# When the first layer's expert weights are fetched: all at once ahead of unit 0, or in five parts beside unit 1

## The chip, the cores and the metric

One core of a Trainium2 chip runs the whole program. The metric is the device time of one execution in microseconds (us), lower is better. "Engine" below means TensorE (PE), VectorE (DVE), ScalarE (ACT), GpSimd (POOL) or SyncE (SP); SP only issues DMA transfers.

## The reference

Two transformer-like layers on x (8 batches of 256 tokens, 256 wide) with a context of 8 x 256 x 192:

- layer 0: x += tanh(g) * cross-attention(layernorm(x), context), 16 heads of 16; then x += tanh(g) * mixture(layernorm(x)), eight experts of inner width 128 of which a token uses four, and one shared expert: `silu(x Wg) * (x Wu) Wd`
- layer 1: the same cross-attention with its own weights, its scores clipped, and a check for NaN; then a mixture of eight experts of inner width 1024, two for each token

The weights that this change moves are layer 0's Wg, Wu and Wd for the eight experts and the shared one, its router's rows and correction bias, and layer 1's attention and router weights.

## The kernel before

Attention is worked through in 16 units, one for each layer and batch. Unit u's scores take eight slots of the program, one for each pair of heads; unit u begins at slot `base(u) = 18 + 8u`. In a slot PE computes one pair's scores by query (L693, `by_query`); DVE takes their row maxima (L1267, `rowmax`), and PE may not overwrite `by_query` before that. When the eight maxima of a unit are there, DVE makes a shift of them, PE turns it (L700), ACT copies it (L1069 and L1070, `shiftT`), and SP sends it on a round trip: `place_shift` stores it to DRAM (L518, `max<-shiftT`), waits, and loads it from there as two more rows of the unit's query stack (L523, `stack_q<-max`). Only then can PE compute that unit's scores by key (L712, `by_key`), ten slots (`LAG`) after its scores by query; ACT exponentiates them (L1077), and PE multiplies them with the values (L730). Projections, layer norms and layer 0's experts (PE L786, L796) of other units are put between these on the same in-order engines.

Before a unit starts, its keys and queries are stored to DRAM in two precisions (L474 and L477 for keys, L485 and L488 for queries; unit 0's queries go by ACT's queue) and loaded back by twelve transfers into stacks (L501 `stack_k<-qk`, L512 `stack_q<-qk`). PE's first `by_query` of a unit waits for them.

The order on each engine is a list written out by hand: `make_plan()` puts stages at half slots, and every engine walks the same plan. SP takes at slot g the stages of half slots 2g-3 and 2g-2, in order, and blocks where it must wait. Almost all DMA of this part is issued by SP, on one queue. SP's order around the change is:

```
slot 18  load(2): x and context of batch 3; all of layer 0's expert weights
slot 19  store of unit 1's queries        slot 21  store of context 2
slot 22  stacks of unit 1                 slot 23  store of unit 2's keys
slot 26  load(3): batch 4; layer 1's attention weights (8 transfers)
slot 27  place_shift(0), store of unit 2's queries
slot 29/30  context 3, stacks of unit 2   slot 31  store of unit 3's keys
slot 34  load(4): batch 5; layer 1's router weights and zero rows (7 transfers)
slot 35  place_shift(1), store of unit 3's queries
slot 37/38  context 4, stacks of unit 3   slot 39  store of unit 4's keys
slot 42  load(5)                          slot 43  place_shift(2), ...
```

`load_experts0` issues 12 transfers on `ffn0_in`: router rows (L425), bias (L426), four of gate and up weights with the shared expert's part behind each (L430, L431), down weights and the shared one (L432, L433). `gate_turn` (PE L765, ACT L1096) turns the router's rows and waits for all of them; it stands in slot 34, and the first experts' matmuls come in slot 44. PSUM banks for all such stages are handed out in turn over three banks, in the plan's order.

Of the kernel before, what the change touches and what calls it, by code (L numbers as in the profile page):

```python
# [21 lines left out]
P = 128  # L22
# [6 lines left out]
KC = D // P  # L29
E0, I0 = 8, 128  # L30
# [22 lines left out]
LAG = 10  # L53
# [12 lines left out]
def layer_of(u):  # L66
    return u // NB
# [6 lines left out]
def base(u):  # L74

    return LEAD + PAIRS * u


def make_plan():

    at = defaultdict(list)
    for u in range(UNITS):
        g = 2 * base(u)
        at[g - 34].append(("load", u))
        if u == 0:
            for i, stage in enumerate(FIRST):
                at[g - 30 + i].append(stage)
        else:
            at[g - 28].append(("ctx", u))
            at[g - 25].append(("kprod", u))  # L90
            at[g - 23].append(("stats", ("query", u)))
            at[g - 21].append(("normal", ("query", u)))
            at[g - 19].append(("turn", ("query", u)))
            at[g - 16].append(("qprod", u))
            at[g - 10].append(("stack_keys", u))
            at[g - 10].append(("stack_queries", u))
        at[g + 13].append(("vprod", u))
        at[g + 16].insert(0, ("shift_turn", u))
        e = g + 2 * LAG + 2
        at[e + 9].append(("take", 2 * u))  # L100
        at[e + 11].append(("turn_values", 2 * u))
        at[e + 17].append(("take", 2 * u + 1))
        at[e + 19].append(("turn_values", 2 * u + 1))
        at[e + 21].append(("attn_turn", u))
        at[e + 23].append(("project", u))
    at[2 * base(0)].append(("out_bias", 0))
    at[2 * base(NB) - 40].append(("scale_queries", 1))
    at[2 * base(2)].append(("gate_turn", 0))
    g = 2 * base(NB)
    at[g].append(("out_bias", 1))  # L110
    at[g + 6].append(("mean_v", 0))
    at[g + 10].append(("mean_turn", 0))
    at[g + 15].append(("mean_project", 0))
    for b in range(NB):
        e = 2 * base(0) + 2 * LAG + 25 + EXPERTS0_STEP * b
        at[e].append(("stats", ("ffn0", b)))
        at[e + 2].append(("normal", ("ffn0", b)))
        at[e + 5].append(("turn", ("ffn0", b)))
        at[e + 6].append(("route0", b))
        at[e + 8].append(("groups0", b))  # L120
        at[e + 9].append(("ranks0", b))
        at[e + 10].append(("weights0", b))
        for n in range(N0):
            at[e + 7 + EXPERTS0_STEP * n // N0].append(("gate_up", N0 * b + n))
            at[e + 12 + EXPERTS0_STEP * n // N0].append(("down0", N0 * b + n))
    g = 2 * base(UNITS - 1)
    at[g - 20].append(("load_alternative", 0))
    at[g - 13].append(("any_nan", 0))
    at[g - 11].append(("spread_nan", 0))
    for b in range(NB):  # L130
        g = 2 * base(UNITS - 1) - 9 + FINISH_STEP * b
        if b >= KEPT_FROM:
            g = max(g, 2 * base(NB + b) + 2 * LAG + 26)
        if b < KEPT_FROM:
            at[g - 9].append(("reload", b))
        at[g].append(("pick_z", b))
        at[g + 2].append(("stats", ("finish", b)))
        at[g + 4].append(("normal", ("finish", b)))
        at[g + 6].append(("turn", ("finish", b)))
        at[g + 8].append(("logits1", b))  # L140
        at[g + 9].append(("soft1", b))
        at[max(g + 10, 2 * base(UNITS) + 1 + b)].append(("count1", b))
        if b == NB - 1:
            at[g + 11].append(("blocks", 0))
            at[g + 12].append(("tables", 0))
        at[g + 11].append(("weights1", b))
        late = 5 if b == NB - 2 else 0
        at[g + 13 + late].append(("bias_turn", b))
        at[g + 15 + late].append(("bias1", b))
    return at  # L150
# [25 lines left out]
def bank_release(stage, n):  # L176

    if stage == "turn":
        return "xnT_ready", NORM_NO[n] + 1
    return {  # L180
        "gate_turn": ("gate_wT_ready", 1), "spread_nan": ("keep_ready", 1),
        "mean_v": ("mean_ready", 1), "mean_turn": ("mean_ready", 2), "mean_project": ("zalt_ready", 1),
    }.get(stage) or {
        "ctx": ("ctxT_ready", n + 1), "kprod": ("k_lo", n + 1), "qprod": ("q_lo", n + 1),
        "vprod": ("v_ready", n + 1), "out_bias": ("obias_ready", 2 * n + 2),
        "bias_turn": ("biasT_ready", n + 1), "bias1": ("x_done", n + 1),
        "shift_turn": ("shiftT_ready", n + 1), "turn_values": ("normal_done", n + 1),
        "attn_turn": ("attnT_ready", n + 1), "project": ("z_ready", n - NB + 1) if layer_of(n) else ("x0_ready", n + 1),
        "route0": ("sig_exp", n + 1), "gate_up": ("h_ready", n + 1), "down0": ("x_acc", n + 1),
        "logits1": ("logits_ready", n + 1),  # L190
    }[stage]


def share_banks():

    bank_of, uses = {}, []
    for g in sorted(PLAN):
        for stage, n in PLAN[g]:
            if stage in ("load", "stack_keys", "stack_queries", "stats", "scale_queries", "normal", "take", "groups0", "ranks0", "weights0", "any_nan",
                         "reload", "load_alternative", "pick_z", "soft1", "count1", "weights1", "blocks", "tables") or (stage == "ctx" and layer_of(n)):  # L200
                continue
            i = len(uses)
            bank_of[stage, n] = (i % 3, bank_release(*uses[i - 3]) if i >= 3 else None)
            uses.append((stage, n))
    return bank_of


BANK_OF = share_banks()


def build(nc, a, out):
    es = ExitStack()
    first = ExitStack()
    sem = Semaphores(*[es.enter_context(nc.semaphore(name)) for name in SEMAPHORES])
# [5 lines left out]
    def sba(name, shape, dt=F32):  # L220
        return first.enter_context(nc.sbuf_tensor(name, shape, dt))
# [50 lines left out]
    w_gate0 = sba("w_gate0", [P, KC, N0, I0])  # L272
    w_up0 = sba("w_up0", [P, KC, N0, I0])
    w_down0 = sba("w_down0", [P, N0, D])
    gate_wT = sba("gate_wT", [P, KC, E0])
    corr = sba("corr", [P, E0])
# [25 lines left out]
    gate_rows = hidden0[2][0:E0, :]  # L302
# [90 lines left out]
    def _(sp):  # L393
        def load_x(b):
            sp.dma_start(x_tiles(b), a["x"][b].rearrange("(t p) d -> p t d", p=P)).then_inc(x_in[b], 16)
# [25 lines left out]
                    sp.dma_start(dst, col.rearrange("(k p) -> p k", p=P),  # L421
                                 allow_slow_non_contiguous=True).then_inc(attn_w_in[l], 16)

        def load_experts0():
            sp.dma_start(gate_rows, a["L0_ffn_gate_w"]).then_inc(sem.ffn0_in, 16)  # L425
            sp.dma_start(corr[:, :], a["L0_ffn_correction_bias"].partition_broadcast(P)).then_inc(sem.ffn0_in, 16)  # L426
            for k in range(KC):
                rows = slice(k * P, k * P + P)
                for t, w, shared in ((w_gate0, a["L0_ffn_Wg"], a["L0_ffn_Wg_s"]), (w_up0, a["L0_ffn_Wu"], a["L0_ffn_Wu_s"])):
                    sp.dma_start(t[:, k, 0:E0, :], w[:, rows, :].rearrange("e p i -> p e i")).then_inc(sem.ffn0_in, 16)  # L430
                    sp.dma_start(t[:, k, E0, :], shared[rows, :]).then_inc(sem.ffn0_in, 16)  # L431
            sp.dma_start(w_down0[:, 0:E0, :], a["L0_ffn_Wd"].rearrange("e i d -> i e d")).then_inc(sem.ffn0_in, 16)  # L432
            sp.dma_start(w_down0[:, E0, :], a["L0_ffn_Wd_s"]).then_inc(sem.ffn0_in, 16)  # L433

        def load_router():
            sp.dma_start(wr[:, :, :], a["L1_ffn_Wr"].rearrange("(k p) e -> p k e", p=P)).then_inc(sem.router_in, 16)
# [18 lines left out]
        def load(u):  # L455
            if layer_of(u):
                reload_context(u)
            if u == 0:
                load_attention_weights(0)
            if u + 1 < NB:  # L460
                load_x(u + 1)
                load_ctx(u + 1)
            if u == 2:
                load_experts0()
            if u == 3:
                load_attention_weights(1)
            if u == 4:
                sp.wait_ge(sem.const, 1)
                load_router()

# [111 lines left out]
        def store_rows(b):  # L582
# [4 lines left out]
        load_x(0)  # L587
        load_ctx(0)
        stages = {"load": load, "ctx": context, "kprod": store_keys, "qprod": store_queries, "stack_keys": stack_keys, "stack_queries": stack_queries,
                  "shift_turn": place_shift, "mean_project": store_alternative, "project": store_z, "reload": reload, "load_alternative": load_alternative,  # L590
                  "weights1": store_rows, "bias1": store_x, "tables": first_weights}
        for g in range(SLOTS_IN_ALL):
            u, p = divmod(g - base(0) - LAG, PAIRS)
# [1201 lines left out]
```

## Time and profile before

| | |
|---|---|
| median of 3 runs | 1070.68 us (1070.47 to 1071.9) |
| the profiled execution | 1065.39 us, its span 1063.6 us |
| busy share of the span | PE 87%, DVE 71%, ACT 46%, POOL 22% |
| mean granted clock of PE | 0.896 of full speed |
| bytes moved | 142.03 MB, mean 134 GB/s |

The profiled execution is one of those of the kernel, 5.3 us under the median of the timed ones; about 1.8 us of it lies outside the span. Shares are averages over stages with different limits; the change moves work that lies in the first 160 us.

### The profile page before, as it was taken

What the parts mean: (1) busy time and instruction counts of PE and PEld (TensorE: products, weight loads), DVE (VectorE), ACT (ScalarE), POOL (GpSimd) and SP (SyncE); (2) the same over time, 40 slices, a digit from 0 to 9 for tenths busy, and PEclk for the clock granted to TensorE, in tenths of its full rate; (3) what the DMA queues carried; (4) which work ended last, traced back from release to release, by engine and by line L of the source; (5) the groups of instructions that cost most, each with busy time, mean ns of one, the idle gap of its engine ahead of it and who ended that gap; (6) DMA issues with size and microseconds to landing.
All of it is one profiled execution on the core that took longest, in us unless ns stands there. A gap on an engine that the chain in (4) does not pass through costs nothing.

```text
span 1063.6 us, 17907 instructions
## 1 busy us (share of the span) xinstructions
PE 922.6 (87%) x6385; PEld 736.5 (69%) x6385; DVE 754.2 (71%) x1489; ACT 486.1 (46%) x842; POOL 235.0 (22%) x386
## 2 busy tenths in 40 slices
PE   3568999999999999898897676785489999999995
PEld 2345677777777676676665444553389999999995
DVE  3634667777667678788867578963768888888882
ACT  2125644444444444334343333442256676667762
POOL 2011211020210000201010122421135444454423
PEclk9557999999999999899998766865589999999998
DMA  6996746056055116365462874341366776677742
GB/s 151 265 176 140 132 78 109 23 95 103 31 84 84 31 55 123 94 120 107 128 124 91 161 150 111 93 131 40 110 239 209 233 233 220 202 227 236 230 140 30
DMA packets 121080, 142.03 MB, mean 134 GB/s; under 512 B 11456, under 2 KB 105304, under 8 KB 120864
## 3 DMA queue, kind: packets, MB, share of 16 engines
q1 hardware_dynamic: 110512, 128.11, 48.5%
q0 software_dynamic: 8832, 12.25, 5.3%
q8 instruction: 51, 0.84, 0.3%
q10 hardware_dynamic: 1648, 0.53, 0.2%
q14 instruction: 37, 0.30, 0.1%
HBM read 109.97 MB, written 30.88 MB: 132 GB/s over the span
## 4 chain that ended last, share of the span: by engine, by line
PE 62%; DVE 14%; DMA 10%; SPq 4%; issue 4%; ACT 3%; POOL 2%; ACTq 0%; POOLq 0%; DVEq 0%
PE bank L947 12%; PE bank L786 8%; PE by_key L931 6%; PE by_query L931 6%; PE bank L796 5%; PE value_bank L730 4%; DVE rowmax L1267 3%; PE by_query L693 3%; PE by_key L712 3%; DMA max<-shiftT 3%; PE bank L640 3%; PE bank L757 3%; PE bank L679 2%; DVE probs L1292 2%; PE bank L649 2%
## 5 line engine op out<-in xcount | busy, mean ns | idle before, releaser
L1267 DVE TENSOR_REDUCE rowmax<-by_query 128x4 f32<-128x1024 f32 x128 | 155.5, 1215 | 27.2 <-PE by_query L693 27.0
L1077 ACT ACTIVATE probs<-by_key 128x1024 f32<-128x1024 f32 x128 | 130.7, 1021 | 66.6 <-PE by_key L712 63.8
L1721 POOL TENSOR_SCALAR rstd<-moments 128x2 f32<-128x2 f32 x32 | 9.6, 300 | 545.6 <-DVE moments L1231 545.6
L1772 POOL DMA_INDIRECT out_x<-x,token_i x46 | 78.2, 1700 | 146.6 <-ACT x L1182 136.6
L693 PE MATMUL by_query<-stack_k,stack_q 48*128 48x256 f32 x512 | 71.0, 359 | 38.3 <-DVE rowmax L1267 20.6
L947 PE MATMUL bank<-w_hi,h_hi 128*128 128x256 f32 x368 | 104.1, 283 | 0.0
L947 PE MATMUL bank<-w_lo,h_hi 128*128 128x256 f32 x368 | 104.1, 283 | 0.0
L947 PE MATMUL bank<-w_hi,h_lo 128*128 128x256 f32 x368 | 104.1, 283 | 0.0
L693 PEld LDWEIGHTS by_query<-stack_k,stack_q 48*128 48x128 f32 x512 | 43.6, 210 | 77.3 <-issue 46.1
L1110 ACT ACTIVATE act_gate<-bank 128x256 f32<-128x256 f32 x72 | 27.6, 383 | 142.4 <-PE bank L786 140.0
L712 PE MATMUL by_key<-stack_q,stack_k 50*128 50x256 f32 x512 | 66.8, 342 | 29.2 <-DMA stack_q<-max 26.3
L1292 DVE SCALAR_TENSOR_TENSOR probs<-probs,lower 128x1024 f32<-128x1024 f32 x64 | 77.8, 1215 | 14.0 <-DMA lower<-max 10.6
L796 PE MATMUL bank<-w_down,hidden 128*128 128x256 f32 x288 | 80.4, 403 | 3.1 <-DVE summed L1324 1.8
L730 PE MATMUL value_bank<-probs,values 128*32 128x256 f32 x1024 | 78.3, 429 | 5.2 <-DVE probs L1292 5.0
L712 PEld LDWEIGHTS by_key<-stack_q,stack_k 50*128 50x128 f32 x512 | 43.6, 209 | 55.9 <-DMA stack_q<-max 28.6
L786 PE MATMUL bank<-xnT,w_gate 128*128 128x256 f32 x288 | 80.0, 401 | 1.7 <-DVE lo L1258 0.5
L1419 DVE SCALAR_TENSOR_TENSOR x<-bank,expert_cols,x 128x256 f32<-128x256 f32 x144 | 62.5, 475 | 21.0 <-PE bank L796 20.9
L786 PE MATMUL bank<-xnT,w_up 128*128 128x256 f32 x288 | 75.9, 387 | 0.0
L947 PEld LDWEIGHTS bank<-w_hi,h_hi 128*128 128x128 f32 x368 | 70.7, 192 | 0.0
L947 PEld LDWEIGHTS bank<-w_lo,h_hi 128*128 128x128 f32 x368 | 70.7, 192 | 0.0
L947 PEld LDWEIGHTS bank<-w_hi,h_lo 128*128 128x128 f32 x368 | 70.7, 192 | 0.0
L1649 DVE TENSOR_TENSOR h_lo<-x,h_hi 128x512 fp32r<-128x512 f32 x92 | 63.7, 693 | 3.2
(228 smaller groups left out, 2141.4 us busy)
## 6 DMA issues: line engine op xcount, KB each, us to landing
w<-in_L_ffn_W SPq DMA_DIRECT2D x46, 1024.0 KB, 8.7
lower<-max SPq DMA_DIRECT2D x64, 256.0 KB, 3.8
stack_k<-qk SPq DMA_DIRECT2D x96, 128.0 KB, 5.0
stack_q<-qk SPq DMA_DIRECT2D x96, 128.0 KB, 7.4
qk<-hi SPq DMA_DIRECT2D x31, 256.0 KB, 3.5
qk<-lo SPq DMA_DIRECT2D x31, 256.0 KB, 4.1
rows<-w_gate SPq DMA_DIRECT2D x8, 264.0 KB, 3.6
x<-in_x SPq DMA_DIRECT2D x8, 256.0 KB, 8.0
```

Source lines behind the costliest of these rows:

```text
L693: mm = pe.matmul(by_query[:, side, t * S:t * S + S], sq[rows, p, t * P:t * P + P], sk[rows, p, :], start=True, stop=True)
L712: mm = pe.matmul(by_key[:, side, kt * S:kt * S + S], sk[rows, p, kt * P:kt * P + P], sq[rows, p, :], start=True, stop=True)
L730: mm = pe.matmul(value_bank[32 * c:32 * c + 32, o:o + S], values[u % 2][:, kt, 4 * j + c, :], probs[(i + c // 2) % 4][:, kt, c % 2, :], st ...
L786: mm = pe.matmul(bank[:, half * S:half * S + S], w[:, k, e, :], turned_of(("ffn0", b))[:, k, :], start=k == 0, stop=k == 1)
L796: mm = pe.matmul(bank[:, t * D:t * D + D], hidden0[i % 6][:, t * P:t * P + P], w_down0[:, e, :], start=True, stop=True)
L931: mm = pe.matmul(up_bank[pair][:, half * SLOTS:half * SLOTS + SLOTS], wt[:, k, j * P:j * P + P], xt[:, k, :], start=n == 0, stop=n == len( ...
L947: mm = pe.matmul(bank[:, t * D:t * D + D], ht[:, j, t * P:t * P + P], wt[:, j, :], start=j == 0 and t == 0 and n == 0, stop=j == JH - 1 an ...
L1077: ac.activation(probs[i % 4][:, :, :, :].rearrange("p k h s -> p h k s"), by_key[:, :, :].rearrange("p h (k s) -> p h k s", k=2), ACT.Exp) ...
L1267: dv.tensor_reduce(rowmax[u % 2][:, 2 * p:2 * p + 2, :], by_query[:, :, :].rearrange("p h (t s) -> p h t s", t=TT), AX, ALU.max).then_inc( ...
L1292: dv.scalar_tensor_tensor(prob, prob, 1.0, bound, ALU.min, ALU.max).then_inc(sem.clip_done, 1)
L1649: dv.tensor_tensor(hl[:, part, :], relu[pair], hh[:, part, :].bitcast(F32), ALU.subtract).then_inc(sem.h_lo, 1)
L1772: po.indirect_dma_start(out[:, :], bass.IndirectOffsetOnAxis(ap=token_i[:, n:n + 1].bitcast(U32), axis=0), ysb[i % 3][:, t, :], None, comp ...
```

## The change

`load_experts0` becomes five parts: gate weights for each half of the rows (part 0 also brings the router's rows and the bias), up weights for each half, down weights. They are put at half slots 59, 61, 63, 65 and 67, so that SP issues them in its slots 31 to 35: part 0 behind the store of unit 3's keys, part 3 ahead of `load(4)`, part 4 ahead of `place_shift(1)`. `gate_turn` goes from half slot 68 to 85. Layer 1's attention weights go from `load(3)` to `load(5)`, its router weights from `load(4)` to `load(6)`.

```diff
     at[2 * base(NB) - 40].append(("scale_queries", 1))
-    at[2 * base(2)].append(("gate_turn", 0))
+    g = 2 * base(1) + 7
+    for i in range(5):
+        at[g + 2 * i].append(("load_experts0", i))
+    at[2 * base(0) + 2 * LAG + 25 + 4].append(("gate_turn", 0))
...
-        def load_experts0():
-            sp.dma_start(gate_rows, a["L0_ffn_gate_w"]).then_inc(sem.ffn0_in, 16)
-            sp.dma_start(corr[:, :], a["L0_ffn_correction_bias"].partition_broadcast(P)).then_inc(sem.ffn0_in, 16)
-            for k in range(KC):
+        def load_experts0(i):
+
+            if i == 0:
+                sp.dma_start(gate_rows, a["L0_ffn_gate_w"]).then_inc(sem.ffn0_in, 16)
+                sp.dma_start(corr[:, :], a["L0_ffn_correction_bias"].partition_broadcast(P)).then_inc(sem.ffn0_in, 16)
+            if i < 2 * KC:
+                up, k = divmod(i, KC)
                 rows = slice(k * P, k * P + P)
...
+                t, w, shared = ((w_up0, a["L0_ffn_Wu"], a["L0_ffn_Wu_s"]) if up else (w_gate0, a["L0_ffn_Wg"], a["L0_ffn_Wg_s"]))
+                sp.dma_start(t[:, k, 0:E0, :], w[:, rows, :].rearrange("e p i -> p e i")).then_inc(sem.ffn0_in, 16)
+                sp.dma_start(t[:, k, E0, :], shared[rows, :]).then_inc(sem.ffn0_in, 16)
+            else:
+                sp.dma_start(w_down0[:, 0:E0, :], a["L0_ffn_Wd"].rearrange("e i d -> i e d")).then_inc(sem.ffn0_in, 16)
+                sp.dma_start(w_down0[:, E0, :], a["L0_ffn_Wd_s"]).then_inc(sem.ffn0_in, 16)
...
-            if u == 2:
-                load_experts0()
-            if u == 3:
+            if u == 5:
                 load_attention_weights(1)
-            if u == 4:
+            if u == 6:
                 sp.wait_ge(sem.const, 1)
                 load_router()
```

The rest of the diff lets `load_experts0` be a stage of SP's list and of none that takes a PSUM bank.

## Rows read from the trace of the kernel before

**Rows 1.** Stretches: length, busy time (count) of PE, PEld, DVE, ACT, POOL; PEclk, DMA share, GB/s.

```profile
24.00:27.00 3.00, 0.00 (x0) 0.00 (x0) 2.15 (x7) 0.22 (x1) 0.62 (x3) 0.97 1.16 129
27.00:30.00 3.00, 0.00 (x0) 0.00 (x0) 2.54 (x2) 1.03 (x2) 1.53 (x6) 0.50 1.13 127
39.00:46.00 7.00, 4.51 (x22) 2.78 (x22) 4.49 (x7) 1.67 (x6) 0.00 (x0) 0.74 1.17 290
48.00:51.00 3.00, 1.88 (x7) 0.83 (x6) 0.81 (x3) 0.84 (x2) 0.00 (x0) 0.50 1.11 366
69.00:70.00 1.00, 0.00 (x0) 0.00 (x0) 0.83 (x3) 0.05 (x1) 0.00 (x0) 1.00 0.36 44
78.00:86.00 8.00, 6.05 (x35) 4.03 (x37) 4.09 (x8) 2.86 (x5) 1.05 (x3) 0.50 1.15 139
88.00:91.00 3.00, 3.00 (x7) 2.45 (x8) 0.84 (x1) 1.58 (x3) 0.71 (x1) 0.50 1.07 343
125.00:150.00 25.00, 24.68 (x164) 18.06 (x161) 18.55 (x52) 11.38 (x22) 3.36 (x9) 1.00 0.69 133
```

**Rows 2.** The chain that ended last, from 26 us on: start, us, what.

```profile
30.43 1.90 SPq L425
...
45.54 7.31 DMA qk<-lo
...
55.11 8.50 DMA stack_q<-qk
...
65.22 5.64 DMA max<-shiftT
```

**Rows 3.** SP's DMA issues in order of time (start, us to issue).

```profile
45.06 0.43 SPq L485 DMA_DIRECT2D qk<-hi  x1
...
70.87 1.36 SPq L523 DMA_DIRECT2D stack_q<-max  x2
...
74.46 2.79 SPq L501 DMA_DIRECT2D stack_k<-qk  x6
...
82.60 0.38 SPq L477 DMA_DIRECT2D qk<-lo  x1
...
87.37 0.64 SPq L442 DMA_DIRECT2D out_x<-zero_row  x1
95.19 0.50 SPq L518 DMA_DIRECT2D max<-shiftT  x1
97.02 1.26 SPq L523 DMA_DIRECT2D stack_q<-max  x2
...
121.31 0.51 SPq L518 DMA_DIRECT2D max<-shiftT  x1
```

**Rows 4.** PE, and one row of DVE, in order of time (in brackets: idle before, releaser).

```profile
30.20 1.08 PE L670 MATMUL bank<-ident,xn 128*128 128x128 f32 x4 [6.92 <-ACT xn L1043]
55.10 3.78 PE L649 MATMUL bank<-wkv,ctxT 96*128 96x256 f32 x8
60.50 1.23 DVE L1267 TENSOR_REDUCE rowmax<-by_query 128x4 f32<-128x1024 f32 x1 [4.06 <-PE by_query L693]
63.71 0.80 PE L693 MATMUL by_query<-stack_k,stack_q 48*128 48x256 f32 x4 [3.25 <-DMA stack_q<-qk]
74.24 0.79 PE L712 MATMUL by_key<-stack_q,stack_k 50*128 50x256 f32 x4 [1.20 <-DMA stack_q<-max]
101.31 0.50 PE L712 MATMUL by_key<-stack_q,stack_k 50*128 50x256 f32 x4
114.99 1.89 PE L649 MATMUL bank<-wkv,ctxT 96*128 96x256 f32 x8
128.83 0.50 PE L712 MATMUL by_key<-stack_q,stack_k 50*128 50x256 f32 x4
```

**Rows 5.** DMA issues by line up to 150 us: count, KB each, median us to landing.

```profile
w_gate<-in_L_ffn_Wg SPq DMA_DIRECT2D x2, 512.0 KB
...
w_down<-in_L_ffn_Wd SPq DMA_DIRECT2D x1, 1024.0 KB
```

More of the change, by code:

```diff
@@ L199, in share_banks @@
             if stage in ("load", "stack_keys", "stack_queries", "stats", "scale_queries", "normal", "take", "groups0", "ranks0", "weights0", "any_nan",
-                         "reload", "load_alternative", "pick_z", "soft1", "count1", "weights1", "blocks", "tables") or (stage == "ctx" and layer_of(n)):
+                         "reload", "load_experts0", "load_alternative", "pick_z", "soft1", "count1", "weights1", "blocks", "tables") or (stage == "ctx" and layer_of(n)):
                 continue
@@ L422, in load_attention_weights @@
                                  allow_slow_non_contiguous=True).then_inc(attn_w_in[l], 16)
-        def load_experts0():
-            sp.dma_start(gate_rows, a["L0_ffn_gate_w"]).then_inc(sem.ffn0_in, 16)
-            sp.dma_start(corr[:, :], a["L0_ffn_correction_bias"].partition_broadcast(P)).then_inc(sem.ffn0_in, 16)
-            for k in range(KC):
-                rows = slice(k * P, k * P + P)
[L429 to L433, printed above, removed]
+        def load_experts0(i):
[4 more added lines that the diff above has]
+                up, k = divmod(i, KC)
+                rows = slice(k * P, k * P + P)
+                t, w, shared = ((w_up0, a["L0_ffn_Wu"], a["L0_ffn_Wu_s"]) if up else (w_gate0, a["L0_ffn_Wg"], a["L0_ffn_Wg_s"]))
[4 more added lines that the diff above has]
+                sp.dma_start(w_down0[:, E0, :], a["L0_ffn_Wd_s"]).then_inc(sem.ffn0_in, 16)
         def load_router():
@@ L589, in _ @@
         stages = {"load": load, "ctx": context, "kprod": store_keys, "qprod": store_queries, "stack_keys": stack_keys, "stack_queries": stack_queries,
-                  "shift_turn": place_shift, "mean_project": store_alternative, "project": store_z, "reload": reload, "load_alternative": load_alternative,
+                  "shift_turn": place_shift, "mean_project": store_alternative, "project": store_z, "reload": reload, "load_experts0": load_experts0, "load_alternative": load_alternative,
                   "weights1": store_rows, "bias1": store_x, "tables": first_weights}
```

## The prediction, as it was put on record

> **What bounds the kernel now.** I read the stretches first, then the chain of waits over the first 130 us, then SP's issues and PE's instructions in order of time. From 125 us on PE is busy 24.68 of 25 us at the full clock [rows 1]: a delay or gain that reaches that point is carried to the end one for one, so only the first 130 us need a sum. There the chain runs through SP and DMA [rows 2]: SP issues expert weights from 30.43 us; the store of unit 1's queries goes out only at 45.06 and 45.54, and its second part takes 7.31 us to land; the query stacks then take 8.50 us. PE begins unit 1's scores at 63.71 after 3.25 us of waiting for them [rows 4]. The shift's first trip takes 5.64 us [rows 2] against 97.02 - 95.19 = 1.83 us for the next unit's [rows 3], and PE waits 1.20 us more for it at 74.24 [rows 4].
>
> The DMA engines have two rates [rows 1]: 139 GB/s while the stacks are loaded (78 to 86 us), 290 where gate and up weights pass (39 to 46), 343 to 366 for transfers of longer rows (88 to 91, 48 to 51). A transfer of one queue that is issued behind others lands behind them.
>
> **What the change removes.** Nothing reaches unit 0's scores: its stacks were issued before the experts. Behind it:
>
> 1. Unit 1's stacks. Their issue no longer stands behind 12 transfers; PE and DVE of unit 0 do not speed up. PE may start unit 1 when DVE has read the last scores of unit 0: 60.50 + 1.23 = 61.73, say 61.9 against 63.71 [rows 4]. Gain 1.8 us, not the 3.25 that PE shows, because DVE is next to be late. The stacks, issued from about 45 us and needing about 13 (unit 2's: 74.46 to some 87, from rows 1 and 3), land near 58 and cover this.
> 2. Unit 0's shift. Issued at 65.22 - 1.8 = 63.4, with no layer 1 weights ahead of it: 1.83 us to land, then from L523 to `by_key` 74.24 - 70.87 = 3.4 [rows 3, 4], so 68.7. PE comes there at 74.24 - 1.20 - 1.8 = 71.2. The 1.20 us goes too: gain so far 3.0 us at slot 28.
>
> Left alone, PE would reach unit 1's first `by_key` (101.31 before, no wait shown [rows 4]) at 98.3, and its shift would be ready for L518 at about 95.19 - 3.0 = 92.2 [rows 3].
>
> **What it adds, step by step.** The 12 issues now come behind unit 3's key store (82.60 before [rows 3]) and ahead of `place_shift(1)`. Before, SP had only the router's seven transfers there and was idle from 88.0 to 95.19 [rows 3]. The data is the larger part:
>
> - Unit 2's stacks are issued at 74.46 - 1.8 = 72.6 (they hang on context 3, ahead of the 1.20 us) and passed in 12.5 us before, until about 87 [rows 1, 3]. So the queue reaches what is behind them at 85.1.
> - Ahead of L518 then lie: unit 3's keys, 0.52 MB; x and context 5, 0.46 MB; gate and up, 4 x (512 + 64) KB = 2.36 MB; down, 1152 KB = 1.18 MB (sizes [rows 5] and the arrays' shapes). 2.36 MB at 290 GB/s is 8.1 us, 2.16 MB at 350 is 6.2 us: 14.3 us, until 99.4.
> - The shift's store lands behind that. The nearest pattern is unit 0's in the kernel before: the queue ran empty at about 69.2 (share 0.36 in 69 to 70 [rows 1]) and `by_key` started at 74.24: 5.0 us. So unit 1's `by_key` starts at 104.4, against 101.31: **+3.1 us**. Bounds: 4.52 MB at 366 with 3.4 us behind it gives 100.9 (-0.4); all at 290 with 5.0 gives 105.7 (+4.4).
> - SP itself has issued the last part some us before its data has passed and is not later than this. While it waits for the shift's store, unit 3's query store, context 4 and unit 3's stacks stand behind it. Before, L523 of unit 1 went out at 97.02; now at about 101. The stacks then land at about 118 us, unit 3 begins at about 122 to 124: covered by 4 us, else late by the excess.
> - PE is in order: while `by_key` waits, from 98.3 to 104.4, unit 2's next scores and unit 4's key projection wait too. The idle time also bears on the clock. Before, PE idled 6.92 us until 30.20 [rows 4]; the granted clock was 0.97 in 24 to 27 and 0.50 (1.2 GHz) in 27 to 30, and it was still 0.50 in 78 to 86 and 88 to 91 with PE busy 6.05 of 8 and 3.00 of 3 us [rows 1]. At that level the eight matmuls of L649 take 3.78 us, at the full clock 1.89 [rows 4]. A 6 us stall at 98 us should bring the fall again. Cost: nothing if the clock holds; at most half of the 9.05 us busy in those two stretches, 4.5 us. I take half of some 3.2 us: **+1.6 us**.
>
> **Costed at nothing.** Layer 1's attention weights in `load(5)`: about 1.06 MB, 3 us of DMA, ahead of unit 2's shift. L518 of that unit went out at 121.31 and its `by_key` ran at 128.83; the round trip takes 1.83 + 3.4 = 5.2, so 2.3 us of cover, and the queue should be empty by 124.5 when the shift comes at 126. Without cover it costs up to 3 us. The router's transfers in `load(6)` fall in the next unit, where DMA is busy 0.69 of the time [rows 1]. `gate_turn`'s own instruction only moves; its weights have landed 15 us earlier. Its PSUM bank is freed at once, and the turn of the first expert input now waits for an older neighbour: at worst a fraction of a microsecond.
>
> **Sum.** -3.0 (two waits gone) + 6.1 (new wait at `by_key`) = +3.1; +1.6 clock; together +4.7 us, bounds -0.4 and +8.9. The profiled execution of 1065.39 us becomes 1070.1; the median of the timed runs lies 5.3 us above it, so 1075.4 us.
>
> **Rivals.**
>
> A, faster: the shift's small store does not wait its turn behind the experts, or SP gets to it before. Then the 3.0 us stays: 1067.7 us. It would need L518's data to pass 3.6 MB already in the queue. Against it: with the layer 1 weights ahead, the same store took 5.64 us instead of 1.83 [rows 2, 3], and unit 1's query store 7.31. It decides if the landing comes before 98.3 - 3.4 = 94.9 us. A page of the Trainium skill, "DMA: Bandwidth & Descriptors", section "Queues, rings and completion order", says that a copy is split over up to 16 engines' rings and that completion is not first in, first out for an issuing engine; by it a later small transfer could land first, which gives this case's 1067.7 us, though the same section has each engine take descriptors in ring order, which gives mine. The two landings just named agree with the latter. Chance 0.17.
>
> B, no change: unit 1's shift is late by only what the front gained: the transfers pass at 366 GB/s and the landing is quick (100.9 to 102 us), and the clock holds. The time stays within 2 us of 1070.7. For it: the bound above, and PE's clock could rise sooner in 62 to 92 us. That would bring unit 2's stacks out sooner, but not what follows the stall. Chance 0.23.
>
> C, the forecast, +2 to +9 us, mostly near +4.7. Chance 0.52.
>
> D, slower by more: unit 3's stacks or unit 2's shift also come too late, each a further 2 to 4 us with a second fall of the clock: 1080 to 1084. It decides if L518 of unit 1 lands after 103 us. Chance 0.08.
>
> **How the numbers follow.** What a measurement of this kernel can tell from no change is about 0.2%, 2.1 us. Faster by more: case A, 0.17. Within: case B, 0.23. Slower: C and D, 0.60. The predicted time is C's 1075.4; C alone lies in 1073 to 1079.5. The range for 8 in 10 leaves out most of A below and D above: 1068 to 1080.
>
> **What the profile of the changed kernel would show.** Right: no wait for `stack_q<-qk` at unit 1's first scores, which start near 61.9; the first `by_key` near 71.2 without a wait; DMA share near 0.2 or less in parts of 38 to 45 us; weight issues from about 80 to 93; a wait of about 6 us of L712 for `stack_q<-max` that ends near 104; a granted clock of 0.50 around or behind it. Wrong: L518 of unit 1 landing within 2 us of its issue, or no wait at slot 36 (then A); unit 1's first scores well before 61.9 would mean that something in unit 0 hung on DMA that I missed; a clock at the full level after the stall makes it +3. A wait at unit 2's `by_key` or unit 3's first scores would be D.

## The result, and the profile after

| | before | changed |
|---|---|---|
| median of 20 runs each | 1069.56 us (1061.1 to 1075.66) | 1073.33 us (1068.98 to 1079.12) |
| the profiled execution | 1065.39 us, span 1063.6 | 1077.79 us, span 1076.0 |
| ratio of the times | | 1.0043, 95% interval [1.0023, 1.0064] |

By the ratio the change makes the kernel 0.43% slower, some 4.6 us (2.5 to 6.8 by the interval); the two medians lie 3.8 us apart. The two profiled executions differ by 12.4 us, more than the timed runs do, so part of that is chance of the single execution, and it has to be told apart below.

In the changed kernel the lines lie five further down for TensorE's and ScalarE's stages: L698 is the scores by query, L717 the scores by key, L523 and L528 SP's shift trip. First PE in order of time (brackets: idle before, releaser). The rows answer to [rows 4].

```profile
62.10 0.80 PE L698 MATMUL by_query<-stack_k,stack_q 48*128 48x256 f32 x4 [1.42 <-DVE rowmax L1272]
...
71.15 0.79 PE L717 MATMUL by_key<-stack_q,stack_k 50*128 50x256 f32 x4
...
98.16 0.64 PE L629 MATMUL bank<-ident,ctx_tok 128*96 128x128 f32 x4
104.84 0.80 PE L717 MATMUL by_key<-stack_q,stack_k 50*128 50x256 f32 x4 [6.03 <-DMA stack_q<-max]
...
109.40 3.78 PE L645 MATMUL bank<-ctxT,wkv 96*128 96x256 f32 x8
...
127.62 0.30 PE L705 MATMUL bank<-ident,shift 128*96 128x128 f32 x1
```

Unit 1's first scores start at 62.10 in place of 63.71, released by DVE; the first `by_key` runs at 71.15 in place of 74.24, without a wait. Then PE stands still for 6.03 us at unit 1's first `by_key`, which before ran at 101.31 with no wait.

SP's issues in order of time, against [rows 3]:

```profile
72.63 2.77 SPq L506 DMA_DIRECT2D stack_k<-qk  x6
...
80.00 0.47 SPq L430 DMA_DIRECT2D hidden<-in_L_ffn_gate_w  x1
...
93.35 1.34 SPq L440 DMA_DIRECT2D w_down<-in_L_ffn_Wd_s  x1
94.73 0.66 SPq L523 DMA_DIRECT2D max<-shiftT  x1
101.55 1.23 SPq L528 DMA_DIRECT2D stack_q<-max  x2
...
129.31 0.51 SPq L523 DMA_DIRECT2D max<-shiftT  x1
```

The weights fill SP from 80.00 to 94.7; the shift's store is issued right behind and lands 6.82 us later (101.55), where it took 1.83 us before. SP also came to the store late: PE turned this shift at 91.91 us, and in the kernel before SP issued the store 0.70 us behind the turn (94.49 to 95.19), so that 2.1 us of the trip's delay passed before the issue and 5.0 us behind it. The stretches (columns as in [rows 1]) show what the DMA engines and the clock did meanwhile:

```profile
38.00:40.00 2.00, 1.60 (x7) 1.03 (x5) 1.95 (x4) 0.84 (x2) 0.00 (x0) 0.88 0.00 0
70.00:73.00 3.00, 2.38 (x14) 1.57 (x12) 1.80 (x2) 1.66 (x5) 0.00 (x0) 0.50 0.00 0
77.00:84.00 7.00, 5.05 (x36) 2.69 (x36) 4.09 (x8) 2.89 (x4) 1.74 (x7) 0.50 1.16 142
88.00:94.00 6.00, 5.83 (x45) 3.85 (x43) 2.86 (x5) 3.03 (x5) 0.00 (x0) 0.86 1.16 292
95.00:99.00 4.00, 3.03 (x33) 1.65 (x32) 3.32 (x6) 1.95 (x3) 0.00 (x0) 1.00 0.98 298
99.00:104.00 5.00, 0.00 (x0) 0.00 (x0) 0.50 (x1) 0.76 (x4) 0.00 (x0) 0.93 0.14 46
104.00:120.00 16.00, 13.51 (x76) 8.41 (x76) 5.84 (x11) 5.54 (x7) 1.65 (x6) 0.50 1.11 212
122.00:130.00 8.00, 7.83 (x59) 5.82 (x57) 4.73 (x11) 5.09 (x10) 2.14 (x8) 1.00 0.27 54
```

The DMA engines are now empty in 38 to 40 and in 70 to 73 us, where nothing uses them, and full from 77 to 99. From 104 to 120 PE runs at the lower level, 1.2 GHz. The eight matmuls of L645 at 109.40 take 3.78 us there; in the kernel before the same stage is L640, at the full clock:

```profile
104.72 1.99 PE L640 MATMUL bank<-ctxT,wkv 96*128 96x256 f32 x8
```

A mark that can be compared from one execution to the next is the start of a unit's shift turn on PE. Unit 3's, in the two profiled executions of each kernel (the second pair was taken later; lines differ by one):

```profile
157.36 0.32 PE L700 MATMUL bank<-ident,shift 128*96 128x128 f32 x1
```
```profile
161.87 0.31 PE L701 MATMUL bank<-ident,shift 128*96 128x128 f32 x1
```
```profile
165.95 0.32 PE L705 MATMUL bank<-ident,shift 128*96 128x128 f32 x1
```
```profile
162.07 0.32 PE L706 MATMUL bank<-ident,shift 128*96 128x128 f32 x1
```

These are before, before again, changed, changed again. The same program reaches this mark 4.5 us or 3.9 us apart in two executions. The means, 159.6 and 164.0, differ by 4.4 us; a single pair of profiles would have said 8.6 or 0.2. With two executions of each kernel, that 4.4 is close to the timed 4.6 is luck and no evidence. The same turns of later units show how far the mark reaches (all in us):

| shift turned | before | before again | changed | changed again |
|---|---|---|---|---|
| unit 1 | 94.49 | 98.75 | 91.91 | 90.36 |
| unit 2 | 119.61 | 124.13 | 127.62 | 123.73 |
| unit 3 | 157.36 | 161.87 | 165.95 | 162.07 |
| unit 9 | 416.95 | 421.46 | 425.54 | 421.65 |
| unit 15 | 680.30 | 682.70 | 691.91 | 687.56 |

From unit 3 to unit 9 all four take 259.6 us, so that a delay of the front is carried on unchanged that far; the prediction had it unchanged to the end. From unit 9 to unit 15 they take 263.4, 261.2, 266.4 and 265.9 us, at a mean granted clock of 0.86, 0.87, 0.85 and 0.85 (420 to 690 us). Two further runs told of below, the 46 matmuls of 48 rows and the shift on ScalarE's queue, have the changed kernel's plan in this stretch and take 262.8 and 262.5 us. So no cost of the change is shown there; it is a second source of scatter, of some 6 us over all profiles.

### The profile page after: what moved, and what is told of

It is laid out like the page before. It is cut to its first block, busy times and chain, and to the rows that moved or that the text cites. A ratio compares the mean times of both kernels' runs of the same rounds, so it can differ in the third digit from the quotient of the medians.

```text
span 1076.0 us, 17907 instructions
## 1 busy us (share of the span) xinstructions
PE 934.7 (87%) x6385; PEld 744.3 (69%) x6385; DVE 754.1 (70%) x1489; ACT 486.4 (45%) x842; POOL 234.3 (22%) x386
## 4 chain that ended last, share of the span: by engine, by line
PE 63%; DVE 15%; DMA 8%; issue 4%; SPq 4%; ACT 3%; POOL 2%; ACTq 0%; POOLq 0%; DVEq 0%
PE bank L952 12%; PE bank L791 8%; PE by_key L936 6%; PE by_query L936 6%; PE bank L801 5%; PE bank L645 4%; PE value_bank L735 4%; DVE rowmax L1272 3%; PE by_query L698 3%; DMA max<-shiftT 3%; PE by_key L717 3%; PE bank L762 3%; PE bank L684 2%; DVE probs L1297 2%; PE bank L654 2%
## 5 line engine op out<-in xcount | busy, mean ns | idle before, releaser
L1272 DVE TENSOR_REDUCE rowmax<-by_query 128x4 f32<-128x1024 f32 x128 | 155.5, 1215 | 32.5 <-PE by_query L698 32.3
L698 PE MATMUL by_query<-stack_k,stack_q 48*128 48x256 f32 x512 | 72.4, 365 | 32.3 <-DVE rowmax L1272 21.0
L717 PE MATMUL by_key<-stack_q,stack_k 50*128 50x256 f32 x512 | 67.8, 347 | 34.8 <-DMA stack_q<-max 31.5
L698 PEld LDWEIGHTS by_query<-stack_k,stack_q 48*128 48x128 f32 x512 | 44.7, 215 | 71.6 <-issue 41.3
L717 PEld LDWEIGHTS by_key<-stack_q,stack_k 50*128 50x128 f32 x512 | 44.6, 213 | 61.8 <-DMA stack_q<-max 33.6
```

The lines of the kernel that those rows point to most:

```text
L698: mm = pe.matmul(by_query[:, side, t * S:t * S + S], sq[rows, p, t * P:t * P + P], sk[rows, p, :], start=True, stop=True)
L717: mm = pe.matmul(by_key[:, side, kt * S:kt * S + S], sk[rows, p, kt * P:kt * P + P], sq[rows, p, :], start=True, stop=True)
L1272: dv.tensor_reduce(rowmax[u % 2][:, 2 * p:2 * p + 2, :], by_query[:, :, :].rearrange("p h (t s) -> p h t s", t=TT), AX, ALU.max).then_inc( ...
```

## The experiments

Each was compared with the kernel before on the same chip. The table's last column is the mark just told; both marks are from one execution each, and scatter as above.

| run | ratio to before, 95% interval | unit 1's first `by_key` | unit 3's shift turned |
|---|---|---|---|
| changed | 1.0043 [1.0023, 1.0064] | 104.84 | 165.95 |
| 46 matmuls of 48 rows in the wait | 1.0067 [1.0040, 1.0094] | 101.86 | 165.53 |
| shift on ScalarE's queue | 1.0081 [1.0055, 1.0108] | 104.81 | 165.75 |
| down weights behind the shift | 0.9997 [0.9973, 1.0020] | 100.61 | 164.16 |
| weights in DMA's gaps | 0.9961 [0.9940, 0.9983] | 95.19 | 156.33 |
| 24 matmuls of 128 rows | 1.0038 [1.0008, 1.0067] | 107.42 | 166.53 |
| gaps, and 12 such matmuls | 1.0004 [0.9980, 1.0027] | 96.94 | 156.21 |
| layer 1's weights alone | 0.9978 [0.9950, 1.0007] | 100.37 | 156.42 |
| all five parts behind the shift | 1.0024 [0.9994, 1.0053] | 95.80 | 161.59 |
| 12 matmuls of 128 rows | 1.0050 [1.0027, 1.0073] | 104.80 | 163.43 |
| gaps, layer 1's weights as before | 0.9980 [0.9949, 1.0010] | 100.82 | 157.46 |

### The data ahead of the shift: down weights behind it

```diff
-    g = 2 * base(1) + 7
-    for i in range(5):
-        at[g + 2 * i].append(("load_experts0", i))
+    for i, g in enumerate((59, 61, 63, 65, 69)):
+        at[g].append(("load_experts0", i))
```

> The changed kernel with part 4 alone (the down weights, 1.18 MB) moved from ahead of unit 1's shift to one slot behind it. Theory (the wait is the data ahead of the shift): 1.18 MB at 290 to 350 GB/s is 3.4 to 4 us less, so by_key starts near 101.3 us after a wait of some 2.5 us; whether the clock still falls is open (2.5 us is shorter than the idle time before the fall at 103); unit 2's shift near 119 to 121, the time 1067 to 1070. Rival (the wait comes from SP reaching the shift late, 94.7 against 92.2 us): by_key moves by no more than those 2.5 us, to 102.3 or later.

```profile
100.61 0.80 PE L716 MATMUL by_key<-stack_q,stack_k 50*128 50x256 f32 x4 [4.80 <-DMA stack_q<-max]
```

From the first issue of unit 2's stacks (72.01 us) to L528's counterpart (97.49) it is 25.5 us, against 28.9 and 27.3 in the two profiles of the changed kernel (72.63 to 101.55, 73.35 to 100.67): 1.8 to 3.4 us less for 1.18 MB less. The wait is 4.80 us and not 2.5, because PE came to it earlier, at 95.8 us, in an execution whose clock had risen sooner. The time is that of the kernel before. Both theories put `by_key` near what came, so its start does not tell them apart; the interval and the time go with the data. SP's own delay is not excluded as a part of the wait: it issued this store at 93.20 us, some 3.6 us after it could have (the shift was turned at 88.93). The clock fell here too, at 98 us, with 4.80 us of waiting.

### Everything behind the shift

```diff
-    g = 2 * base(1) + 7
     for i in range(5):
-        at[g + 2 * i].append(("load_experts0", i))
+        at[69].append(("load_experts0", i))
```

> The changed kernel with all five parts behind unit 1's shift and unit 3's query store, ahead of context 4 and unit 3's stacks. Theory (whatever stands behind 3.5 MB in SP's queue is late by its 11 to 12 us, less its cover): unit 1's first by_key does not wait; unit 3's stacks land 11 to 12 us later than they would, and unit 3's first scores by query wait for stack_q some 3 to 4 us. The front's 3 us are spent again: ratio 0.998 to 1.003. Rival (only the shift's round trip is so sensitive): no wait at unit 3, ratio 0.994 to 0.997.

```profile
121.23 0.57 PE L697 MATMUL by_query<-stack_k,stack_q 48*128 48x256 f32 x4 [3.27 <-DMA stack_q<-qk]
```

Unit 1's `by_key` does not wait (95.80 us), and unit 3's first scores wait 3.27 us for their stacks, as the sum said. The 3.5 MB cost whoever stands behind them. The clock fell here as well, in 97 to 98 us, with no DMA wait of PE ahead of it. The ratio's interval includes 1.

### Another queue for the shift

In place of SP, ScalarE issues unit 1's store and, once it has landed, the two loads:

```diff
+            if u == 1:
+                ac.wait_ge(sem.shiftT_ready, 2)
+                ac.dma_start(max_dram[0][1, 0:2 * H * TT], shiftT[0:2 * H * TT, :]).then_inc(sem.shift_out, 16)
+                ac.wait_ge(sem.shift_out, 32)
...
+                    ac.dma_start(stack_q[1][o:o + 2, :, :].bitcast(F32), src[side]).then_inc(sem.shift_in, 16)
```

> The changed kernel, with unit 1's shift trip (the store and the two loads) issued by ScalarE on its own queue in place of SP's; the expert weights are where the change put them. Theory (the shift waits its turn behind 4.5 MB in SP's queue, as in order of issue): on another queue it lands within 2 to 3 us although the expert weights still pass, unit 1's first by_key starts near 99 us with less than 2 us of waiting, no fall of the clock, unit 2's shift is turned at 117 to 119 us, and the time is 1065 to 1068. ScalarE stands still for some 3 to 4 us meanwhile. Rival (the bandwidth itself is short, whatever the queue): the store still takes 5 to 7 us, by_key starts near 104 us or later, and the time is 1073 or more.

```profile
92.16 0.60 ACTq L1080 DMA_DIRECT2D max<-shiftT  x1
96.75 1.81 ACTq L1085 DMA_DIRECT2D stack_q<-max  x2
```

The store took 4.59 us: 2.2 less than on SP's queue behind the weights, 2.8 more than the 1.83 of an empty queue. So both were half right: the order of the queue is one part, the other is that the same DMA engines are full. The Trainium skill ("DMA: Bandwidth & Descriptors", section "Queues, rings and completion order") has each DMA engine take turns between queues. The 4.59 us are in agreement with it: a store that is shortened on its own queue and not freed. This trip did not hold up unit 1's `by_key`, but ScalarE stood still from 92.8 to 98.7 us and with it PE's previous pair (5.47 us for `probs`), so the stall only changed its place. The clock fell at 99.7 us, and the ratio is the highest of all runs.

### The clock

Four runs put work into the wait or near it; the matmuls write the bank that the next `by_key` overwrites. In the first three PE's wait for ScalarE's exponentials, which read that bank, is moved ahead of the wait for the shift, so that the extra work comes between the two.

```diff
+            if u == 1 and p == 0:
+                for n in range(46):
+                    pe.matmul(by_key[:, 0, 0:S], sk[0:FULL, p, 0:P], sq[0:FULL, p, :], start=True, stop=True)
```

> This is the changed kernel with 46 extra matmuls in slot 36, into the by_key bank that unit 1's first scores by key overwrite anyway, so that PE works while it waits for unit 1's shift; nothing else moves. My theory (a 6 us wait for the shift, and the fall of the clock behind it costs about as much again): the wait's end stays near 104.8 us, the granted clock stays at the full level from 90 us on, unit 2's shift is turned near 123.3 us in place of 127.6, some 4 us earlier, and the time is 1069 to 1070 against 1073.3 (ratio to before 0.999 to 1.000). Rival (the clock falls for another reason, the light load of slots 36 to 38): the clock falls all the same behind the extra work, unit 2's shift is turned near 127 us, and the time stays at 1073.

```profile
94.00:96.00 2.00, 2.00 (x19) 2.00 (x18) 0.39 (x1) 0.65 (x4) 0.00 (x0) 0.94 0.96 298
96.00:98.00 2.00, 2.00 (x11) 2.00 (x11) 0.00 (x0) 0.00 (x0) 0.00 (x0) 0.50 0.31 104
...
110.00:116.00 6.00, 5.09 (x37) 3.16 (x36) 4.61 (x10) 2.89 (x4) 0.88 (x3) 0.50 1.13 212
```

PE was busy without a gap and the clock fell all the same, at 96 us, while 48-row matmuls ran. My expectation failed; unit 2's shift was turned at 127.19 us, as the rival had it. Then with 128 rows of the array in use (`wq` by `wo`), 24 of them. They differ from the first kind in a second thing: the stacks are declared float32r, `wq` and `wo` plain float32, and the trace has one instruction for a matmul of the first kind and two for one of the second. Which of the two decides on the clock was not tried.

> The changed kernel with 24 extra matmuls of 128 rows and 128 columns by 256 in slot 36, where the earlier try had 46 of 48 rows, which did not hold the clock. If it is the kind of load that the clock answers to, it stays at the full level through the wait and beyond 104 us, unit 2's shift is turned 29 us or less behind the end of the wait less some 6 (near 123.5 us where it was 127.6 and 127.2), and the time is 3 to 4 us under the changed kernel's: ratio to before 1.000 to 1.002. Rival (the clock falls at that moment whatever PE does): a fall at 96 to 103 us, unit 2's shift near 127, ratio 1.004 to 1.008 as with the 48-row matmuls.

```profile
96.00:98.00 2.00, 1.95 (x13) 1.71 (x14) 1.23 (x2) 0.75 (x4) 0.00 (x0) 1.00 0.45 150
98.00:104.00 6.00, 6.00 (x29) 5.28 (x29) 0.00 (x0) 0.08 (x1) 0.00 (x0) 1.00 0.53 155
104.00:110.00 6.00, 5.07 (x38) 3.85 (x40) 1.23 (x1) 1.31 (x2) 0.00 (x0) 1.00 1.14 159
110.00:116.00 6.00, 4.16 (x38) 2.88 (x32) 2.39 (x5) 3.08 (x5) 0.00 (x0) 1.00 0.81 154
116.00:122.00 6.00, 6.00 (x41) 3.97 (x38) 3.45 (x7) 3.54 (x5) 3.35 (x9) 0.57 0.94 261
```

The clock stayed at the full level to 116 us. But I had priced a matmul at 0.24 us, and each is two of the trace's, 10.53 us for the 24: they ended at 107.4. The shift's store had landed at 98.39, and `by_key` can follow that by 3.3 us (101.55 to 104.84 in the changed kernel), so the matmuls outlasted the wait by some 5.7 us, and that ate what the clock gave. The clock then fell at 117 us, and the ratio, 1.0038, is not what I expected. With half as many (`range(12)`):

> The changed kernel with 12 of the 128-row matmuls in slot 36. With 24 the clock stayed at the full level through the wait, but they took 10.53 us and outlasted it by some 5.5 us. Twelve take 5.3 us, less than the wait. Theory (the wait's empty time brings the fall): full clock until 110 us or later, unit 1's by_key at 101.7 to 104.8 us as the landing has it, unit 2's shift turned 18.5 to 21 us behind it (22.8 and 20.0 in the two profiles of the changed kernel), ratio 0.999 to 1.002 against 1.0043. Rival: the fall comes all the same, ratio 1.003 or more.

```profile
98.00:104.00 6.00, 2.90 (x14) 2.21 (x12) 0.00 (x0) 0.00 (x0) 0.00 (x0) 1.00 0.34 110
104.00:110.00 6.00, 4.44 (x30) 2.56 (x31) 1.22 (x1) 2.48 (x3) 0.00 (x0) 0.52 1.09 213
110.00:116.00 6.00, 4.16 (x32) 3.06 (x31) 2.72 (x6) 1.91 (x4) 0.00 (x0) 0.91 1.15 151
```

They filled 5.35 us; 3.90 us of wait were left, and at 104 us the clock fell, but was back at 111. From `by_key` to unit 2's shift turn it is 20.3 us (104.80 to 125.10), as expected, but the clock did not stay at the full level until 110 us, and the timed ratio, 1.0050, is not better than the changed kernel's. So what the fall costs in the timed runs is not shown.

To see whether the fall belongs to the change at all, both kernels were profiled again, unchanged.

> The kernel before once more, unchanged, for a second profile. Open after the first runs: the granted clock fell at 96 to 103 us in all five profiles of kernels with the experts moved, with a wait or without, and not in the one profile of the kernel before. If the fall belongs to those kernels, it is absent here too: unit 2's shift is turned 25.1 us behind unit 1's, as in the first profile. Rival (it belongs to the light load of slots 36 to 38, and the first profile escaped it by the moment of its earlier rise): the clock falls here as well in slots 36 to 38, and unit 2's shift is turned 28 to 30 us behind unit 1's.

> The changed kernel once more, unchanged, for a second profile. Theory (the wait is fixed by the data in SP's queue): unit 1's first by_key starts 32 to 32.5 us behind the first issue of unit 2's stacks (32.2 in the first profile) after a wait of some 6 us, whatever the clock did before. The fall of the clock behind it is expected again; how long it lasts (17 us in the first profile) may differ by one step of 3 to 4 us.

In the kernel before the clock did not fall in slots 36 to 38 this time either, with its light load there: before, unit 2's shift came 25.1 us behind unit 1's, now 25.4 (98.75 to 124.13). But it had risen late, at 99 us, where it rose at 91 in the first profile. That is only a part of the 4.5 us that this execution is behind the first: 2.0 us were there at unit 0's first scores (36.44 against 34.44) and 2.3 at unit 1's (65.99 against 63.71).

```profile
96.00:98.00 2.00, 2.00 (x20) 0.58 (x16) 1.49 (x4) 1.02 (x1) 0.00 (x0) 0.50 0.00 0
98.00:104.00 6.00, 5.69 (x47) 4.06 (x47) 3.06 (x6) 3.02 (x7) 0.00 (x0) 0.88 0.09 25
```

In the changed kernel, the wait was there again, 6.46 us, 30.35 us behind the first stack issue (32.2 in the first profile). I had expected 32 to 32.5, so the data passed 1.9 us faster than the theory of a fixed time allows:

```profile
103.70 0.80 PE L718 MATMUL by_key<-stack_q,stack_k 50*128 50x256 f32 x4 [6.46 <-DMA stack_q<-max]
```

and the clock was down for some 10 us (99.3 to 109.5) where it had been 17 (103.3 to 120.4). Of the 3.9 us between the two marks, 1.1 are the earlier `by_key` and 2.8 the way from there to unit 2's shift turn, which holds the shorter fall.

### Layer 1's weights alone

The kernel before, with only `u == 3` and `u == 4` in `load` made 5 and 6.

> The kernel before with layer 1's attention and router weights alone moved two units later; the expert weights stay at once ahead of unit 0. Theory (the two waits of the front have separate causes): PE's wait for unit 1's query stacks stays (unit 1's first scores near 63.7 us), the first trip of the shift takes 2 us in place of 5.64, the first by_key starts 1.2 us earlier with no wait; unit 1's by_key does not wait. Time 1 us under before, ratio 0.997 to 1.000. Rival (moving them costs something at unit 2's shift): a wait of L717's counterpart at unit 2, or no gain at all.

```profile
63.82 0.80 PE L693 MATMUL by_query<-stack_k,stack_q 48*128 48x256 f32 x4 [3.27 <-DMA stack_q<-qk]
...
73.26 0.80 PE L712 MATMUL by_key<-stack_q,stack_k 50*128 50x256 f32 x4
```

The wait for unit 1's stacks is unchanged, the shift's store lands in 1.87 us (65.32 to 67.19), and the 1.20 us wait is gone. The two waits of the front have separate causes, one for each half of the change. The ratio's interval, 0.9950 to 1.0007, just includes 1.

### The weights in DMA's gaps

```diff
-    g = 2 * base(1) + 7
-    for i in range(5):
-        at[g + 2 * i].append(("load_experts0", i))
+    for i, g in enumerate((37, 37, 47, 55, 69)):
+        at[g].append(("load_experts0", i))
```

> The changed kernel with the five parts where its trace shows the DMA engines idle: parts 0 and 1 at half slot 37 (behind the store of unit 1's queries, 41 to 45 us), part 2 at 47 (ahead of 60 us), part 3 at 55 (behind unit 2's query store, 69 to 72 us), part 4 at 69 (behind unit 1's shift). Theory: the 3.0 us of the front are kept (unit 1's first scores at 62 us, the first by_key at 71.2 without a wait), unit 1's first by_key starts near 98.3 us without a wait for the shift, no fall of the clock, unit 2's shift is turned near 117 us (119.6 before, 127.6 changed), and the time is about 3 us under before: 1066 to 1067, ratio 0.996 to 0.998. Rival (the early transfers hold up unit 1's stacks again): a wait at 62 us and half or less of the gain, unit 2's shift at 118.5 or later.

Its stretches (PE to GB/s as above):

```profile
38.00:46.00 8.00, 5.28 (x23) 3.55 (x23) 4.33 (x7) 1.67 (x6) 0.00 (x0) 0.71 0.53 149
66.00:71.00 5.00, 2.68 (x16) 2.07 (x16) 3.23 (x4) 0.89 (x6) 0.00 (x0) 0.50 0.76 223
92.00:97.00 5.00, 3.51 (x36) 2.00 (x36) 3.77 (x6) 2.96 (x7) 0.00 (x0) 1.00 0.78 228
...
98.00:104.00 6.00, 6.00 (x28) 3.55 (x30) 0.00 (x0) 1.98 (x3) 0.00 (x0) 0.50 1.14 194
```

The stretches that were empty now carry the weights; unit 1's first scores start at 61.60 and its first `by_key` at 95.19, neither with a DMA wait. It is the fastest version: 0.9961 [0.9940, 0.9983] against before, some 4 us. Its interval overlaps that of layer 1's weights alone (0.9978), so what the expert weights add to the gain is not told by time. I expected no fall of the clock, and it fell, at 97 us, with no DMA wait ahead of it; the mark is at 156.33 in spite of that. Here the matmuls with which the clock had stayed up were tried as well, three ahead of each of unit 1's first four `by_key`:

> The kernel with the weights in DMA's gaps (ratio 0.996), with three extra matmuls of 128 rows ahead of each of unit 1's first four by_key pairs, where PE waits some 0.3 to 0.9 us for ScalarE. They cost at most 12 x 0.24 = 2.9 us at the full clock, some of it inside waits. If the load of slots 36 to 38 decides on the clock, it no longer falls at 97 us and unit 2's shift is turned 26 to 28 us behind unit 1's (29.6 without them): 1 to 3 us gained, ratio 0.993 to 0.996. Rival (no hold on the clock): it falls all the same, the extra work costs 3 to 6 us, ratio 0.998 to 1.001.

Unit 2's shift was turned 29.0 us behind unit 1's (29.6 without them), the mark stayed (156.21) and the timed ratio was 1.0004: they cost what they gave or more. But the clock did not fall. The same stage without them and with them, and a stretch with them:

```profile
99.76 3.78 PE L644 MATMUL bank<-ctxT,wkv 96*128 96x256 f32 x8
```
```profile
101.56 1.99 PE L644 MATMUL bank<-ctxT,wkv 96*128 96x256 f32 x8
98.00:104.00 6.00, 5.37 (x39) 3.60 (x39) 0.95 (x1) 2.55 (x4) 0.00 (x0) 1.00 1.13 202
```

The granted clock was full from 85 to 128 us. The clock had risen at 83 to 84 us in both. So, as far as one execution of each shows, a load of this kind in slots 36 to 39 keeps this fall away. The fall's price can be read too: 29.6 us from turn to turn with it, 25.1 and 25.4 in the kernel before without it, some 4.2 to 4.5 us. The twelve matmuls took 6.1 us of PE.

With layer 1's weights put back where the kernel before has them:

> The kernel with the parts in DMA's gaps (ratio 0.9961), but layer 1's attention and router weights where the kernel before has them (units 3 and 4's loads). Theory: the attention weights (1.06 MB, issued ahead of unit 0's shift) delay that shift as before, and part 3, which used the gap at 67 to 71 us, comes on top; the first by_key waits 1 to 3 us; the router's small transfers cost nothing. Ratio 0.998 to 1.000, some 1 to 3 us over the version with both moved. Rival (layer 1's weights do not matter): ratio 0.995 to 0.997.

```profile
73.65 0.80 PE L716 MATMUL by_key<-stack_q,stack_k 50*128 50x256 f32 x4 [3.03 <-DMA stack_q<-max]
```

The first `by_key` waits 3.03 us, as the theory had it, and the ratio is 0.9980, with an interval that includes 1. It also overlaps the interval of the version with both moved, so the time alone does not show what layer 1's weights cost. This run has the experts moved, and the clock did not fall; unit 2's shift came 25.2 us behind unit 1's:

```profile
98.00:104.00 6.00, 4.70 (x56) 2.71 (x56) 4.18 (x6) 3.35 (x7) 0.00 (x0) 1.00 0.86 273
```

So the fall does not belong to every kernel with the experts moved. Six profiles have no extra work and no wait of PE of a microsecond or more in slots 35 to 38. In four of them (before, before again, layer 1's weights alone, this one) the clock had risen at 90 to 99 us and did not fall in slots 36 to 38; in two (the weights in DMA's gaps, all five parts behind the shift) it had risen at 83 to 84 us and fell at 97. The changed kernel's front, which brings PE to these slots earlier, may bring the fall by that; no run shows it alone.

## Why the prediction was right, point by point

- **Unit 1's stacks, 1.8 us, not 3.25.** 61.9 forecast, 62.10 measured, and DVE was what released it. The step that mattered was to ask what is late next.
- **Unit 0's shift.** First `by_key` at 71.2 forecast, 71.15 measured; the run with layer 1's weights alone shows which half of the change did it.
- **The new wait.** Forecast from 98.3 to 104.4; measured from 98.8 to 104.84, and to 103.70 in the second profile. Queue order and full engines both enter: on its own queue the store still took 4.59 us. The prediction told of queue order only, and its sum, drain of the queue at 99.4 us and then 5.0 us, was right for the pair of them: the DMA share is 0.98 until 99 us and 0.14 behind it, and `by_key` follows that by some 5.5 us in the first profile and 4.3 in the second. From the first issue of unit 2's stacks to the landing it takes 27.3 to 29.2 us in the five profiles with this placement and SP's queue, whenever PE arrives; a PE that comes earlier only waits longer.
- **-3.0 + 6.1 = +3.1.** At unit 1's `by_key`: 104.84 and 103.70 against 101.31 in the first profile of before, +3.5 and +2.4. Against the second profile of before (105.82) it is less than nothing, since there the clock had risen late; the timed runs, not a pair of profiles, carry the sign. The 3.0 us of the front rest on the first profile of before in the same way: at unit 1's shift turn the changed kernel is 2.6 to 8.4 us ahead, by the pair that is taken.
- **The clock, +1.6.** The fall came where forecast, and its bound was 4.5 us. No row gives the 3.2 us of which the prediction took half. In the first profile it lasted 17 us and L645 took 3.78 us against 1.99 before (L640); from `by_key` to unit 2's shift turn it took 22.8 us there and 20.0 in the second, against 18.3 in both of before (101.31 to 119.61, 105.82 to 124.13): +4.5 and +1.7. But the reason that I gave, idle time, is not the whole one: the clock also fell with PE busy on 48-row matmuls, and in two versions without a DMA wait. With matmuls of `wq` by `wo` in these slots it stayed up, so the kind of load enters; the rise at 83 to 84 or at 90 us and later may enter too. Twelve such matmuls in the wait shortened the fall without a gain in the timed runs. What the term is worth in those, and what brings the fall in the changed kernel, stays open.
- **Unit 3.** Forecast to begin at 122 to 124; its first scores by query start at 127.18 and 123.29 in the two profiles, without a wait for its stacks. The later one is that with the long fall of the clock.
- **Costed at nothing.** Layer 1's weights at unit 2: `by_key` waits for them in no run, but the cover was used: the shift's store took 3.5 us with layer 1's weights alone and 3.6 with twelve matmuls in the wait, against 1.84 in the changed kernel. `gate_turn`: from unit 2's shift turn to unit 3's it is 37.75 us before (119.61 to 157.36) and with layer 1's weights alone, and 38.33 in the changed kernel; its own instruction now lies in this stretch (0.29 us), and the turn of the first expert input waits 0.30 us for DVE. So it costs 0.6 us, the fraction of a microsecond that was named.
- **The rivals.** A did not come: the small store did wait. B did not come either: the store landed at 101.55, `by_key` at 104.84 and 103.70 was behind B's 100.9 to 102, and the clock fell. D's first mechanism did not come in the change, but is real: with all parts behind the shift, unit 3's stacks were 3.27 us late.
- **The size.** +4.7 us forecast, +0.43% of 1069.56 = 4.6 us measured, 3.8 by the medians. As a time 1075.4 us was forecast and 1073.33 measured; 1.1 us of that is the starting point, a median of three runs that lay above that of twenty. That the change came out within 0.1 us is in part luck: the clock term was a guess between 0 and 4.5, and showed both 4.5 and 1.7.

## What to carry to other kernels

A bulk load that is taken out of one wait has to be paid behind some other latency-critical transfer: write down which small transfers come after its new place, how much data will lie ahead of each, and how much cover each has. Here 4.5 MB ahead of a 32 KB round trip, 3.5 of them the moved weights, made PE wait 6.0 us where the front had gained 3.0, and the same weights in stretches where the DMA engines stood empty brought no wait. Where two executions of one program differ by 4 us at the same mark, a pair of profiles shows the mechanism and the timed runs show the sign.

## What the runs showed of the hardware that was not expected

- 46 float32r matmuls of 48 rows by 128 columns, with PE busy 2.00 of 2 us, did not keep the granted clock: it fell from the full level to 0.50 at 96 us and was still there at 116. With 24 plain float32 matmuls of 128 rows, busy 6.00 of 6 us, it was 1.00 from 96 to 116 us, and with three ahead of each of four `by_key` it did not fall where it had fallen without them. Rows and data type were changed together.
- The clock of the kernel before rose at 91 us in one execution and at 99 in another; that of the changed kernel, once it had fallen, came back after 17 us in one and 10 in another. Two executions of one program are 4.5 or 3.9 us apart by unit 3's shift turn, and the stretch from unit 9's to unit 15's turn scatters by some 6 us more; the timed runs of the kernel before spread over 14.6 us.
- A 32 KB store took 1.83 us with the DMA engines empty, 4.59 on a queue of its own beside expert weights at 290 to 355 GB/s, and 6.82 behind them on theirs (5.83 in the second profile).
